# Coarser ScalarE instructions and other hands for the last squares in a distance attention stage

## The reference

```python
sq = q2 + swapaxes(k2, -1, -2) - 2.0 * einsum('bhqd,bhkd->bhqk', Q, K)
dist = sqrt(maximum(sq, 0.0))
W = (SHEP_EPS + dist) ** (-2)            # SHEP_EPS = 1e-4
W = W / (SHEP_EPS + sum(W, axis=-1, keepdims=True))
A = einsum('bhqk,bhkd->bhqd', W, V)      # then G * A, W_out and the bias
```

## Time and profile before

| | |
|---|---|
| median of 3 runs | 6727.22 us (6725.59 to 6727.43) |
| the profiled execution | 6725.54 us |
| its span, first to last instruction | 6723.8 us |
| ScalarE busy | 6201.9 us, 92% |
| VectorE busy | 5992.2 us, 89% |
| GpSimd busy | 4220.0 us, 63% |
| TensorE busy | 3935.0 us, 59% |
| the first batch's Ln starts at | 255.04 us |
| the last head's L907 ends at | 2205.77 us |

### The profile page before, as it was taken

The page is one execution under the profiler, slowest core; times in us unless marked ns, Lnnn a source line. Parts: engine busy times, 40 slices in busy tenths (PEclk is TensorE's granted clock), DMA queues, the critical chain, the costliest instruction groups (busy, mean ns, idle before and its releaser), DMA issues. The chain is left out here.

```text
span 6723.8 us, 50123 instructions
## 1 busy us (share of the span) xinstructions
PE 3935.0 (59%) x17072; PEld 1381.8 (21%) x17072; DVE 5992.2 (89%) x5936; ACT 6201.9 (92%) x2171; POOL 4220.0 (63%) x1130
## 2 busy tenths in 40 slices
PE   5777777777776674455445455444545444544545
PEld 3222222222222431111111111111111111111213
DVE  7877777777877579999999999999999999999997
ACT  3699999999999249999999999999999999999996
POOL 0399999999999005555656565656555565656563
PEclk8889988988888785656566655565555665566657
DMA  4311111111110430000000000000000000000003
GB/s 149 96 27 20 27 26 26 27 25 22 27 25 15 175 107 6 8 15 9 8 8 15 9 11 13 9 8 8 15 9 15 8 9 8 14 10 8 15 6 103
DMA packets 448856, 191.96 MB, mean 29 GB/s; under 512 B 348038, under 2 KB 429849, under 8 KB 446698
## 3 DMA queue, kind: packets, MB, share of 16 engines
q1 hardware_dynamic: 448618, 188.89, 11.0%
HBM read 112.52 MB, written 76.28 MB: 28 GB/s over the span
## 5 line engine op out<-in xcount | busy, mean ns | idle before, releaser
L1298 POOL TENSOR_TENSOR work<-work 128x1776 f32<-128x1776 f32 (+3 forms) x696 | 2149.9, 3089 | 55.6
L1090 PE MATMUL psS<-q_stack,k_stack 96*128 96x512 bf16 x2048 | 1036.4, 609 | 1753.6 <-DVE work L1206 1687.6
L957 POOL TENSOR_TENSOR work<-work 128x4096 f32<-128x4096 f32 x252 | 1770.9, 7061 | 175.7 <-ACT work L867 175.7
L877 DVE TENSOR_SCALAR work<-psS 128x1024 f32<-128x1024 f32 x1024 | 1198.2, 1218 | 439.6 <-PE psS L778 438.2
L1295 POOL TENSOR_SCALAR work<-work 128x1776 f32<-128x1776 f32 (+2 forms) x174 | 291.2, 1673 | 1980.2 <-ACT work L1180 1972.9
L1201 DVE TENSOR_SCALAR work<-psS 128x1024 f32<-128x1024 f32 x1024 | 1205.2, 1219 | 41.1 <-PE psS L1090 17.3
L1206 DVE TENSOR_TENSOR work<-psS,work 128x1024 f32<-128x1024 f32 x1024 | 1201.4, 1215 | 0.0
L1212 DVE SCALAR_TENSOR_TENSOR work<-work 128x2048 f32<-128x2048 f32 x512 | 1139.3, 2286 | 29.5 <-ACT work L1176 29.5
L1172 ACT ACTIVATE work<-work 128x2048 f32<-128x2048 f32 (+2 forms) x259 | 910.7, 3565 | 54.2 <-DVE work L1206 54.0
L1180 ACT ACTIVATE work<-work 128x6144 f32<-128x6144 f32 (+2 forms) x174 | 907.9, 5218 | 32.2 <-DVE work L1212 32.2
L1176 ACT ACTIVATE work<-work 128x2048 f32<-128x2048 f32 (+1 forms) x343 | 916.0, 2741 | 1.0
(11 more groups left out here) (139 smaller groups left out, 3584.9 us busy)
## 6 DMA issues: line engine op xcount, KB each, us to landing
qk_parts<-work SPq DMA_DIRECT2D x64, 384.0 KB, 3.3
q_stack<-qk_parts SPq DMA_DIRECT2D x384, 64.0 KB, 2.3
k_stack<-qk_parts SPq DMA_DIRECT2D x384, 64.0 KB, 2.3
xT_store<-work SPq DMA_DIRECT2D x2, 4096.0 KB, 15.3
v_store<-work SPq DMA_DIRECT2D x16, 512.0 KB, 3.5
v_tile<-v_store SPq DMA_DIRECT2D x64, 128.0 KB, 2.8
ffn_in<-xT_store SPq DMA_DIRECT2D x64, 128.0 KB, 2.7
y_store<-ffn_out SPq DMA_DIRECT2D x64, 128.0 KB, 2.3
```

Of the source, the lines that this page charges most:

```text
L877: nc.vector.tensor_scalar(lane(g)[:, 0, half * 1024:(half + 1) * 1024], m.psS[half][:, :], ZERO_SHIFT, None, ALU.max).then_inc(s_gd, 1)
L957: nc.gpsimd.tensor_tensor(lane(g, 2), lane(g, 2), lane(g, 2), ALU.mult).then_inc(s_wp, 1)
L1090: last = nc.tensor.matmul(m.psS[half][:, q * 512:(q + 1) * 512], m.k_stack[b][0:ROWS, kt * P:(kt + 1) * P], m.q_stack[b][0:ROWS, c:c + 512 ...
L1298: nc.gpsimd.tensor_tensor(part, part, part, ALU.mult).then_inc(s_pp, 1)
```

## The change

ScalarE's instructions now cover one to six units. `log_cuts` and `inv_cuts` give, for each size of batch, how a pass is cut; a batch of 12 has its Ln in 6, 3 and 3 units and its Sigmoid in 3, 3 and 6. The first two batches have 3 and 9 units where they had 4 and 8. VectorE squares all of the last fourteen units, in six pairs and two single units, and GpSimd stops at unit 497. VectorE does three of these pairs, then the `beside` steps that finish head 30, then the other squares, then the rest.

```diff
-    sizes = [4, 8] + [BATCH] * ((TOTAL - 20) // BATCH) + [8]
+    sizes = [3, 9] + [BATCH] * ((TOTAL - 20) // BATCH) + [8]
...
-    dve_squares = range(TOTAL - 14, TOTAL, 4)
-    pool_squares = [g for g in range(0, TOTAL, 2) if g not in dve_squares]
+    log_cuts = {3: (3,), 9: (3, 6), 12: (6, 3, 3), 8: (3, 3, 2)}
+    inv_cuts = {3: (3,), 9: (3, 6), 12: (3, 3, 6), 8: (2, 2, 2, 1, 1)}
+    FIRST_DVE = TOTAL - 14
+    dve_squares = [(g, 2) for g in range(FIRST_DVE, TOTAL - 2, 2)] + [(TOTAL - 2, 1), (TOTAL - 1, 1)]
+
+    def cut(i, widths):
+        at = starts[i]
+        for n in widths[sizes[i]]:
+            yield at, n
+            at += n
...
-                pair = g - g % 2
-                if pair in dve_squares:
-                    pe.wait_ge(s_wd, dve_squares.index(pair) + 1)
+                if g >= FIRST_DVE:
+                    pe.wait_ge(s_wd, next(i for i, (at, n) in enumerate(dve_squares) if at <= g < at + n) + 1)
                 else:
-                    pe.wait_ge(s_wp, pool_squares.index(pair) + 1)
+                    pe.wait_ge(s_wp, g // 2 + 1)
...
-                for g in range(starts[i], starts[i + 1], 2):
-                    act.wait_ge(s_gd, 2 * (g + 2))
-                    nc.scalar.activation(lane(g, 2), lane(g, 2), ACT.Ln, scale=1.0 / (SHEP_EPS * SHEP_EPS))\
-                        .then_inc(s_ln, 2)
+                for g, n in cut(i, log_cuts):
+                    act.wait_ge(s_gd, 2 * (g + n))
+                    nc.scalar.activation(lane(g, n), lane(g, n), ACT.Ln, scale=1.0 / (SHEP_EPS * SHEP_EPS))\
+                        .then_inc(s_ln, n)
...
-                for g in range(starts[i], starts[i + 1], 2):
-                    act.wait_ge(s_ln, g + 2)
-                    nc.scalar.activation(lane(g, 2), lane(g, 2), ACT.Sigmoid, scale=-0.5).then_inc(s_sg, 2)
+                for g, n in cut(i, inv_cuts):
+                    act.wait_ge(s_ln, g + n)
+                    nc.scalar.activation(lane(g, n), lane(g, n), ACT.Sigmoid, scale=-0.5).then_inc(s_sg, n)
...
-            def squares(g):
-                dve.wait_ge(s_sg, g + 2)
-                nc.vector.tensor_tensor(lane(g, 2), lane(g, 2), lane(g, 2), ALU.mult).then_inc(s_wd, 1)
+            def squares(g, n):
+                dve.wait_ge(s_sg, g + n)
+                nc.vector.tensor_tensor(lane(g, n), lane(g, n), lane(g, n), ALU.mult).then_inc(s_wd, 1)
...
-            for g in dve_squares:
-                squares(g)
-            for g in range(TOTAL, TOTAL + KT + 6):
+            for g, n in dve_squares[:3]:
+                squares(g, n)
+            for g in range(TOTAL, TOTAL + 6):
+                beside(g)
+            for g, n in dve_squares[3:]:
+                squares(g, n)
+            for g in range(TOTAL + 6, TOTAL + KT + 6):
                 beside(g)
...
-            for g in pool_squares:
+            for g in range(0, FIRST_DVE, 2):
```

## The result

The changed kernel takes 6705.45 us (median of 7 runs, 6704.2 to 6706.07) against 6727.22 for the kernel before, measured beside it. The ratio is 0.9968, 95% interval 0.9959 to 0.9978. Forecast were 6706.5 us and a range of 6692 to 6718.

The account below looks back on a forecast made before the run. ScalarE was taken to bound the distance stage. The terms -24.8 + 14 + 1.3 + 6.0 - 17.2 sum to -20.7 us, from 6727.2 to 6706.5 us; range 6692 to 6718 us.

Parts of the forecast that it names:

- Part 1: Distance stage, ScalarE: fewer, longer instructions save 0.10 us each, 0.61 us a round; -24.8 us to batch 42's Sigmoid.
- The rule of the Trainium skill: Rival on ScalarE's instructions: the fixed time is saved in full, by this rule -45 us instead of -24.8; chance 0.02.
- Part 2: Distance stage: GpSimd's later start and Ln's lumped requests make ScalarE wait for unit 11; +14 and +1.3 us.
- Kind A: Ten batches (6, 10, ... 42) where L907 falls after unit 9; ScalarE waits 1.4 us in each, +14 us.
- Kind B: Ten batches (5, 9, ... 41), L907 after unit 5; two, 21 and 33, wait 0.7 us each, +1.3 us.
- batch 25: Batch left 0.1 us to catch the gap before GpSimd's next square; may turn into a miss, 0.7 us more.
- Part 3: Start of the distance stage: later first Ln, and the six-unit Ln waits for unit 11's guard; +6.0 us.
- Part 4: End of the distance stage, from batch 42's Sigmoid: last L907 ends at +64.7 us instead of +81.9; -17.2 us.
- The rival of a slowdown by L907 in every kind of batch: L907 misses a GpSimd square in the other kinds too; 29 batches give +119 us, 6825 us; chance 0.04.

## Why the prediction was right

It was right in its mechanism and in its parts. The errors of the parts are up to 2 us; that the parts as measured sum to -20.7 us, just what was forecast, is luck, since part 1 brought 2.1 less and parts 2 and 4 made up for it.

- **Part 1, ScalarE's instructions: -24.8 forecast, -22.7 measured.** The mechanism holds: the saving is the fixed part of the start-to-start spacing. The size was off by 0.05 us a round: 0.56 instead of 0.61. A six-unit instruction takes 10.43 to 10.45 where the line gave 10.42, a whole pass 20.87 instead of 20.85, and the old pass was read as 21.15 in one row and 21.16 in others. The rule of the Trainium skill (VectorE: DVE Perf Modes, The TRN2 errata) by which it would have been 45 us doesn't hold for this saving: the stretch without waits is 22.7 us shorter, with 243 instructions fewer in it.
- **Part 2, the waits: +15.3 forecast, +13.9 measured.** Kind A: ten waits as forecast, 0.6 to 1.37 us each, 12.0 together where I had 14. Five of them show the full 1.37 or 1.36; in the others unit 11 came up to 0.8 us earlier. Kind B: one wait of 0.64 us (batch 33) instead of two of 0.7; batch 21's L914 caught the gap this time, and batch 25 did not flip. The experiments that move GpSimd's start by -1.7 and +5.2 us and the one that moves L907 show the cause. That the loss per wait is 0.1 more than the gap had no place in the forecast.
- **Part 3, the start: +6.0 forecast, +6.0 measured**, with the gap of 5.3 us where it was placed.
- **Part 4, the end: -17.2 forecast, -17.9 measured.** TensorE did the last unit in 1.06 us where I had put 1.66: its granted clock was 1.00 from 2182 to 2184 us, the higher of its two levels (2.4 GHz), and 0.66 in the stretch of the kernel before from which I took 1.66 (2148 to 2153). TensorE's wait for head 30's copy is 7.7 us, about 10 had been said. Which half does what was not in the prediction: by itself the order of VectorE's queue brings twice as much as the change of hands (11.7 us against 5.1).
- **The sum.** The spans differ by 19.6 us, of which 1.4 of the other sign lie ahead of the stage and have no cause in the change; the runs' medians differ by 21.8, and 20.7 was forecast. The rival of a slowdown by L907 in every kind of batch didn't come. The kernel with the later GpSimd start is slower by nearly as much as that rival would be, with 118.7 us of waits, but not by its mechanism alone: batch 4 waits 2.16 us with L907 nowhere near.

## What to carry to other kernels

When an engine is the bound, merging its instructions saves only the fixed part of the spacing between starts (0.1 us each here), and it delays the first result of a pass and lumps what the pass asks for. Look for who starts on that first result: a small first piece and large later ones (2, 4, 6) keep the saving and give the consumer its start. Before work is shared between engines at the end of a stage, read the in-order queues behind it: here a short copy queued behind four squares cost more than the choice of the engine that did them.

## What the runs showed of the hardware

A VectorE product that reads two tiles in SBUF doesn't run beside a GpSimd product on SBUF. L907 takes 0.42 us with GpSimd idle and up to 7.1 beside it, and it ends within 0.3 us of GpSimd's running square. This I had read from the trace of before; new is how the last squares follow from it. VectorE alone does squares of two units in 4.4 us (the mean of the last three in the changed kernel; its single units take 2.3), while each of GpSimd's between them had added its whole 7.0. VectorE's guards, which read PSUM, take 1.22 us beside GpSimd as without it. The Trainium skill states this (SBUF — State Buffer, Who interferes with whom: the shared port pair is an exclusive lock, held for the full instruction), and the trace agrees with both numbers.

ScalarE's straight line holds to six units, 12288 elements a partition: 10.43 us.

The stage's first guard starts between 250.23 and 253.58 us in the twelve kernels' profiles, though no edit touches what is ahead of it. So the spans of single profiles can't be compared below 3 us. Their stretches from a common event can: from batch 2's Ln to batch 42's Sigmoid it is 1819.74 to 1819.82 us in the four kernels with the old cuts.
